# Flamingo block on one core: the seam between attention and experts, re-ordered by halves

## The chip, the cores and the metric

The kernel runs on 1 core of a Trainium2 chip. The metric is the device time of one execution in microseconds (us), taken as the median of several runs. The engines are TensorE (PE in the profile; PEld are its weight loads), VectorE (DVE), ScalarE (ACT), GpSimd (POOL) and SyncE (SP), which issues most DMAs.

## The reference, cut to what matters

```python
# x, ctx: (16, 256, 512); Wq (512, 512), Wkv (512, 1024); 8 experts, w1, w2, w3: (8, 512, 512)
x = x + tanh(g_xattn) * attention(layernorm(x) @ Wq, ctx @ Wkv)        # one head, softmax over 256 keys
xn = layernorm(x)
probs = softmax(xn @ gate_w + gate_b, axis=1)                          # over the TOKENS of a batch
vals, idx = top_k(probs, 2)                                            # two best experts of each token
y = relu(relu(relu(xn @ w1[e] + b1[e]) @ w2[e] + b2[e]) @ w3[e] + b3[e])
v[e, o] = sum over tokens of y * vals where e is chosen                # per batch and expert, see below
out = sum over chosen e of v[e]                                        # v sums over all 16 batches
x = x + tanh(g_ffn) * out
```

All products are computed in about full float32 precision: each operand is split into a high part (rounded by ScalarE, names `..._hi`) and a low part (`..._lo`, the rest, a subtraction), and three matmuls (hi·hi, hi·lo, lo·hi) are added up in PSUM.

## The kernel before

**Attention phase.** It runs as a software pipeline over 16 batches of 256 tokens. In step b each engine works on several batches at once: `scores(b)`, `gate_transposes(b-2)`, `values(b)`, `ranks(b-2)`, `xn2_transposes(b-1)`, `x_times_a(b+1)`, `gate_logits(b-1)`, `p_times_v(b)`. The gate of a batch is a chain over engines: `gate_logits` (PE), `gate_softmax` (DVE, with the exponential `gate_exp` on ACT), `gate_transposes` (PE), `two_best` (DVE: the two best experts of each token), `ranks` (PE), `slots` (DVE: the slot of each token in its expert's list), `send_pairs` (POOL: four indirect DMAs that write (token, weight) pairs to DRAM).

**Expert phase.** The tokens are taken in tiles of 352 rows that all belong to one expert. For each tile the rows' indices are loaded (`load_idx`, SP), the rows are gathered (`gather`, POOL, three indirect DMAs), transposed on PE (`row_transposes`) into `et`, split (`et_high` on ACT, `et_low` on DVE), and run through three layers (`layer1_half`, `layer2_half`, `layer3_half`: two halves of 24 matmuls of 352 columns each), with `relu_half` on ACT between them and `h_lo` as the low part of the hidden rows. Weights are split once for each tile: `split_w` on ACT, `w_low` on DVE, each over 128x2048 elements. From tile 2 on the tiles run in a loop.

**The table.** Which expert and which rows a tile has is worked out by DVE from the running counts: an early table for 8 tiles once 12 batches are counted (`early_table`, in step 14, 15 dependent steps), the full one in `full_table` (20 steps). The engines read it with a register load (`tiles_in_use`).

**The seam.** The order of every engine between the last attention step and the tile loop is written out by hand. PE: `scores(15)`, `gate_transposes(13)`, `values(15)` with `ranks(13)` inside, `pt_transposes(15)`, `xn2_transposes(14)`, `row_transposes(0)`, `p_times_v(15)`, `gate_logits(14)`, `layer1_half(0, 0)`, `gate_transposes(14)`, `layer1_half(0, 1)`, `row_transposes(1)`, `layer2_first()`, `ranks(14)`, `xn2_transposes(15)`, `layer2_half(0, 1)`, `gate_logits(15)`, `layer1_half(1, ·)`, `gate_transposes(15)`, `row_transposes(2)`, `layer3_half(0, 0)`, `ranks(15)`, `layer3_half(0, 1)`. An engine never overtakes: it waits on semaphores in this order. In DVE's list, `et_low(0)`, `w_low(0, 0)`, `gate_softmax(14)`, `attended(15)`, `w_low(1, 0)`, `two_best(14)`, `et_low(1)`, `slots(14)`, `w_low(0, 1)`, `gt_low(15)`, `w_low(2, 0)`, `gate_softmax(15)`, `w_low(1, 1)` follow one another. In POOL's list stand `gather(1)`, `send_pairs(13)`, `norm2_scale(15)`, `h_low(0, 0)`, `gather(2)`, `send_pairs(14)`, `h_low(1, 0)`, `h_low(0, 1)`. `norm2_scale(15)` gives ScalarE the factors for `norm2(15)`, behind which stand `et_high(1)` and `split_w(0, 1)`.

Before the attention phase the product of Wq and Wk is formed in four steps over c: PE waits for `wq_hi`, `wk_hi`, then for `wq_lo` (DVE), `wk_lo` (POOL). Its matmul lines are 1350 (hi·hi) and 1355, 1356. DVE's line 933 is the helper `low` (every subtraction that gives a low part); PE's lines 1321 to 1323 are the helper `split_product`; 1521 to 1523 are `layer2_first`; 1335 `xn2_transposes`; 1393 `ranks`; 1443 `gate_logits`; 1461 `gate_transposes`; 1576 `row_transposes`.

## Time and profile before

| | |
|---|---|
| median of 3 runs | 938.21 us (937.06 to 938.34) |
| the profiled execution | 939.05 us, its span 937.2 us |
| PE busy | 914.1 us, 98% of the span |
| DVE, ACT, POOL busy | 716.1, 496.1, 277.3 us |
| mean granted TensorE clock | 0.984 |

The span runs from the first to the last instruction; the profiled execution's own time is 1.85 us longer. A row of a timeline gives start, duration, engine, line and operation, then what is written and read, and in brackets the engine's idle time before it with what ended it. Rows whose matmuls overlap are counted by their starts: one begins every 0.16 us at full clock for 352 columns. "Granted clock" 1.00 is 2.4 GHz, 0.50 is 1.2 GHz.

### The profile page before, as it was taken

The page shows a single profiled execution, that of the slowest core. Times are in us where ns is not written, and L with a number is a line of the kernel's source. Part 1 is how long each engine was busy: PE and PEld are TensorE (multiplying, and loading weights), DVE is VectorE, ACT ScalarE, POOL GpSimd, SP SyncE. Part 2 cuts the span into 40 slices and gives each one's busy share as a digit, 9 for nine tenths or more (in the row PEclk, how much of TensorE's full clock was granted, in tenths as well). Part 3 has the DMA queues.
Part 4 walks back from the last instruction along what each step waited for, and adds up shares of the span by engine and source line. Part 5 has one row for each costly group of instructions (what it writes and reads, how often), then busy time and mean ns, then how long its engine had stood idle before and what let it go on. Part 6 is the DMA issues. An engine that isn't in the chain of part 4 may idle for free.

```text
span 937.2 us, 18798 instructions
## 1 busy us (share of the span) xinstructions
PE 914.1 (98%) x5746; PEld 861.3 (92%) x5746; DVE 716.1 (76%) x1369; ACT 496.1 (53%) x690; POOL 277.3 (30%) x316
## 2 busy tenths in 40 slices
PE   9999999999999989999999999999999999999985
PEld 6989988889989878999999999999999999999981
DVE  5667877888778876977777777777777777777756
ACT  5345444454444366556666666666666666666521
POOL 4224444435454557743211111111111111110003
PEclk9999999999999998999999999999999999999995
DMA  7423232223322354447866789973663653752009
GB/s 237 158 100 126 98 128 90 90 98 126 102 99 68 96 148 115 109 124 208 217 206 161 200 239 249 255 224 108 153 198 108 158 192 108 179 172 78 17 17 358
DMA packets 91925, 138.68 MB, mean 148 GB/s; under 512 B 28528, under 2 KB 56944, under 8 KB 88688
## 3 DMA queue, kind: packets, MB, share of 16 engines
q1 hardware_dynamic: 84464, 120.86, 43.1%
q0 software_dynamic: 7424, 17.38, 7.0%
q8 instruction: 18, 0.29, 0.1%
q14 instruction: 19, 0.16, 0.1%
HBM read 106.66 MB, written 31.53 MB: 147 GB/s over the span
## 4 chain that ended last, share of the span: by engine, by line
PE 88%; DVE 4%; DMA 2%; issue 2%; POOL 2%; ACT 1%; SPq 0%; DVEq 0%; POOLq 0%; ACTq 0%
PE bank L1321 27%; PE bank L1322 27%; PE bank L1323 27%; DVE x_all L1311 2%; PE bank L1335 1%; PE bank L1404 1%; DMA xg<-xn_dram,idx 1%; DMA idx<-slot_pair 1%; PE bank L1445 1%; DMA wq_raw<-in_wq_t 1%; POOL slot_pair L634 1%; PE bank L1447 0%; POOL xg L664 0%; DVE probs L1018 0%; PE bank L1576 0%
## 5 line engine op out<-in xcount | busy, mean ns | idle before, releaser
L1321 PE MATMUL bank<-h_hi,w_hi 128*128 128x352 f32 x744 | 241.4, 324 | 1.1 <-issue 1.1
L1323 PE MATMUL bank<-h_hi,w_lo 128*128 128x352 f32 x744 | 240.1, 323 | 0.0
L1322 PE MATMUL bank<-h_lo,w_hi 128*128 128x352 f32 x744 | 239.1, 321 | 0.0
L664 POOL DMA_INDIRECT xg<-xn_dram,idx x72 | 89.6, 1244 | 361.6 <-DMA idx<-slot_pair 346.4
L933 DVE TENSOR_TENSOR w_lo<-w_raw,w_hi 128x2048 fp32r<-128x2048 f32 x72 | 166.4, 2310 | 23.3 <-ACT w_hi L821 18.8
L832 ACT ACTIVATE h<-bank,bias 128x352 f32<-128x352 f32 x192 | 95.8, 551 | 141.5 <-PE bank L1323 139.8
L821 ACT ACTIVATE w_hi<-w_raw 128x2048 fp32r<-128x2048 f32 x72 | 137.4, 1909 | 36.4 <-PE bank L1323 33.0
L1321 PEld LDWEIGHTS bank<-h_hi,w_hi 128*128 128x128 f32 x744 | 139.8, 188 | 1.5 <-issue 1.4
L933 DVE TENSOR_TENSOR h_lo<-h,h_hi 128x704 fp32r<-128x704 f32 x86 | 76.3, 888 | 83.6 <-ACT h_hi L838 83.5
L1322 PEld LDWEIGHTS bank<-h_lo,w_hi 128*128 128x128 f32 x744 | 139.7, 188 | 0.0
L1323 PEld LDWEIGHTS bank<-h_hi,w_lo 128*128 128x128 f32 x744 | 139.3, 187 | 0.0
L1321 PE MATMUL bank<-et_hi,w_hi 128*128 128x352 f32 x384 | 124.0, 323 | 1.3 <-DVE et_lo L933 1.3
L1322 PE MATMUL bank<-et_lo,w_hi 128*128 128x352 f32 x384 | 123.0, 320 | 0.0
L1323 PE MATMUL bank<-et_hi,w_lo 128*128 128x352 f32 x384 | 123.0, 320 | 0.0
L634 POOL DMA_INDIRECT slot_pair<-pair,slot_u x64 | 69.2, 1082 | 40.2 <-DVE pair L990 23.3
L838 ACT ACTIVATE h_hi<-h 128x704 fp32r<-128x704 f32 x96 | 76.3, 794 | 5.5 <-PE bank L1447 1.7
L1321 PEld LDWEIGHTS bank<-et_hi,w_hi 128*128 128x128 f32 x384 | 72.0, 188 | 1.6 <-DVE w_lo L933 1.6
L1322 PEld LDWEIGHTS bank<-et_lo,w_hi 128*128 128x128 f32 x384 | 72.1, 188 | 0.0
L1323 PEld LDWEIGHTS bank<-et_hi,w_lo 128*128 128x128 f32 x384 | 72.0, 187 | 0.0
L1321 PE MATMUL bank<-xt_hi,a_hi 128*128 128x256 f32 x240 | 69.1, 288 | 0.0
L1323 PE MATMUL bank<-xt_hi,a_lo 128*128 128x256 f32 x240 | 67.9, 283 | 0.0
L1322 PE MATMUL bank<-xt_lo,a_hi 128*128 128x256 f32 x240 | 67.9, 283 | 0.0
(215 smaller groups left out, 1735.6 us busy)
## 6 DMA issues: line engine op xcount, KB each, us to landing
w_raw<-in_w SPq DMA_DIRECT2D x24, 1024.0 KB, 5.2
xq<-rows_dram SPq DMA_DIRECT2D x80, 176.0 KB
w_raw<-in_w SPq DMA_DIRECT2D x48, 256.0 KB, 6.7
rows_dram<-xg SPq DMA_DIRECT2D x20, 512.0 KB, 3.3
wb<-slot_pair SPq DMA_DIRECT2D x24, 352.0 KB, 4.0
xt_raw<-in_x_t SPq DMA_DIRECT2D x16, 512.0 KB, 4.0
c_raw<-in_ctx_t SPq DMA_DIRECT2D x16, 512.0 KB, 3.4
x_all<-in_x SPq DMA_DIRECT2D x16, 512.0 KB, 4.5
```

The source lines that it names most:

```text
L634: pool.indirect_dma_start(slot_pair, bass.IndirectOffsetOnAxis(ap=slot_u[:, k, n:n + 1], axis=0), pair[:, k, n], None).then_inc(pair_sent[ ...
L664: pool.indirect_dma_start(xg[0:n, c], None, rows, bass.IndirectOffsetOnAxis(ap=idx[0:n, c, 0:1], axis=0)).then_inc(gathered, 16)
L821: act.activation(w_hi[n][:], w_raw[n][:], ACT.Copy).then_inc(w_his[n], 1)
L832: act.activation(h[:, oc], layer_banks(n, m)[oc][:, 0:TILE], ACT.Relu, bias=bias[n][:, oc:oc + 1]).then_inc(relu_done[n], 1)
L838: act.activation(h_hi[n][:, 2 * k:2 * k + 2], h[:, 2 * k:2 * k + 2], ACT.Copy).then_inc(h_his[n], 1)
L933: dve.tensor_tensor(dst, src, hi.bitcast(F32), ALU.subtract).then_inc(done, 1)
L1311: dve.tensor_tensor(row, bank[n % 8][:], row, ALU.add).then_inc(res_dve, 1)
L1321: pe.matmul(out_ap, lh, rh, start=(i == 0), stop=False)
L1322: pe.matmul(out_ap, lh, rl, start=False, stop=False)
L1323: last = pe.matmul(out_ap, ll, rh, start=False, stop=(i == n - 1))
L1335: last = pe.transpose(banks[dc // 2][:, (dc % 2) * S + c * P:(dc % 2) * S + (c + 1) * P], src[:, c, dc * P:(dc + 1) * P], ident[:])
L1404: last = pe.transpose(bS[:, k * S + c * P:k * S + (c + 1) * P], pexp[:, c, k * P:(k + 1) * P], ident[:])
```

## The change

1. **Seam, tile 0.** `h_low(0, 0)` moves from POOL to DVE (`h_rest`). w1 and w2 of tile 0 are split by halves of the contraction: `split_first_w` on ACT (w1 only), `first_w_low` on DVE (w1 and w2). `layer1_half(0, 0)` becomes `layer1_first`, which goes through the contraction by halves, as `layer2_first` did, and both wait for a half at a time. DVE's `w_low(1, 0)`, then, is `first_w_low(1, 0)`, `h_rest` half 0, `first_w_low(1, 1)`, `h_rest` half 1.
2. **PSUM banks.** Layer 1 of tile 0 uses bank 6 in place of 3, `row_transposes(1)` bank 3 in place of 6, and the waits follow.
3. **Gate.** The biased low logits (`logit_low`) are made by ACT (`gate_low`), the maximum comes out negated in one step, and `two_best` reads PSUM itself and compares the integer indices: 6 steps for 8. This holds for all batches.
4. **Tables.** `early_table` stands behind `two_best(12)` and has 11 steps for 15, `full_table` 17 for 20; three constant tables are made at the start of the kernel on DVE.
5. **Tile 3.** `et_low(3)` stands ahead of `w_low(0, 3)`.
6. **Start.** ScalarE makes `wk_hi[n]` before `wq_hi[n]`.

```diff
         def layer_banks(n, m):
-            first = {(0, 0): (0, 1, 2, 3), (0, 1): (4, 5, 6, 0), (1, 0): (0, 1, 2, 3),
+            first = {(0, 0): (0, 1, 2, 6), (0, 1): (4, 5, 6, 0), (1, 0): (0, 1, 2, 3),
...
-            first = {0: (1, 2, 0), 1: (4, 5, 6), 2: (1, 2, 3)}
+            first = {0: (1, 2, 0), 1: (4, 5, 3), 2: (1, 2, 3)}
...
@@ POOL, seam
             norm2_scale(B - 1)
-            h_low(0, 0)
             gather(2)
...
@@ ACT
+            def gate_low(m):
+                act.wait_ge(gate_done, m + 1)
+                act.activation(logit_low[:], R_LOGIT_LOW, ACT.Identity, bias=gb[:, 0:1]).then_inc(gate_low_done, 1)
...
                 if exists(b - 1, B):
+                    gate_low(b - 1)
                     gate_exp(b - 1)
...
             for n in range(DC):
+                act.wait_ge(s_wk_in[n], 16)
+                act.activation(wk_hi[:, n], wk_raw[:, n], ACT.Copy).then_inc(s_wk_hi, 1)
                 act.wait_ge(s_wq_mean, n + 1)
                 act.activation(wq_hi[:, n], wq_raw[:, n], ACT.Identity, bias=wq_mean[:, n, 1:2]).then_inc(s_wq_hi, 1)
-                act.wait_ge(s_wk_in[n], 16)
-                act.activation(wk_hi[:, n], wk_raw[:, n], ACT.Copy).then_inc(s_wk_hi, 1)
...
+            def split_first_w(k):
+
+                act.wait_ge(w_in[0], W_IN[0])
+                act.activation(w_hi[0][:, 2 * k:2 * k + 2], w_raw[0][:, 2 * k:2 * k + 2], ACT.Copy
+                               ).then_inc(w_first_hi if k == 0 else w_his[0], 1)
...
             et_high(0, range(2))
-            split_w(0, 0)
+            split_first_w(0)
             et_high(0, range(2, TH))
+            split_first_w(1)
+            gate_low(B - 2)
             gate_exp(B - 2)
...
             split_w(1, 1)
+            gate_low(B - 1)
             gate_exp(B - 1)
...
@@ DVE, gate_softmax
-                need(dve, gate_done, m + 1)
-                dve.tensor_scalar(logit_low[:], R_LOGIT_LOW, gb[:, 0:1], None, ALU.add).then_inc(gate_step, 1)
-                dve.wait_ge(gate_step, 3 * m + 1)
+                dve.wait_ge(gate_low_done, m + 1)
                 dve.tensor_tensor(logit[:], R_LOGIT, logit_low[:], ALU.add).then_inc(gate_step, 1)
...
+                dve.tensor_reduce(gmax[:], logit[:], AX_X, ALU.max, negate=True).then_inc(gmax_ready, 1)
...
@@ DVE, step 14
-                if isinstance(b, int) and b == KNOWN + 2:
-                    early_table()
                 if exists(b - 2, B):
                     two_best(b - 2)
+                if isinstance(b, int) and b == KNOWN + 2:
+                    early_table()
...
@@ DVE, seam
+            def first_w_low(n, k):
+
+                dve.wait_ge(w_first_hi if (n, k) == (0, 0) else w_his[n], 1)
+                low(w_lo[n][:, 2 * k:2 * k + 2], w_raw[n][:, 2 * k:2 * k + 2], w_hi[n][:, 2 * k:2 * k + 2],
+                    w_first_lo if k == 0 else w_los[n])
...
             et_low(0, range(2))
-            w_low(0, 0)
+            first_w_low(0, 0)
             et_low(0, range(2, TH))
+            first_w_low(0, 1)
             gate_softmax(B - 2)
             attended(B - 1)
-            w_low(1, 0)
+            first_w_low(1, 0)
+            h_rest(0, 0, [0])
+            first_w_low(1, 1)
+            h_rest(0, 0, [1])
             two_best(B - 2)
...
             w_low(1, 2)
+            et_low(3)
             w_low(0, 3)
-            et_low(3)
...
@@ PE
+            def layer1_first():
+
+                need(pe, et_los, TH)
+                for k in range(2):
+                    pe.wait_ge(w_first_lo if k == 0 else w_los[0], 1)
+                    for oc in range(2):
+                        z = layer_banks(0, 0)[oc][:, 0:TILE]
+                        rows = slice(oc * P, (oc + 1) * P)
+                        for i in range(2 * k, 2 * k + 2):
+                            pe.matmul(z, w_hi[0][:, i, rows], et_hi[:, i], start=(i == 0), stop=False)
+                            pe.matmul(z, w_hi[0][:, i, rows], et_lo[:, i], start=False, stop=False)
+                            last = pe.matmul(z, w_lo[0][:, i, rows], et_hi[:, i], start=False, stop=(i == DC - 1))
+                last.then_inc(l_done[0], 1)
...
             gate_logits(B - 2)
-            layer1_half(0, 0)
+            layer1_first()
             gate_transposes(B - 2)
             layer1_half(0, 1)
```

## Rows read from the trace of the kernel before

**Rows 1.** Busy time by stretch: PE, PEld, DVE, ACT, POOL; granted clock, DMA share, GB/s.

```profile
320.00:360.00 40.00, 35.48 (x206) 31.85 (x204) 26.76 (x76) 19.68 (x32) 24.08 (x26) 0.91 0.62 170
...
480.00:880.00 400.00, 400.00 (x2500) 400.00 (x2499) 312.25 (x388) 243.56 (x279) 56.45 (x48) 1.00 0.61 170
```

**Rows 2.** Timeline of the kernel's start: DVE, PE.

```profile
7.58 0.69 DVE L1162 TENSOR_REDUCE wq_mean<-wq_raw 128x1 f32<-128x512 f32 x1 [0.80 <-DMA wq_raw<-in_wq_t]
...
11.30 0.47 PE L1355 MATMUL bank<-wk_lo,wq_hi 128*128 128x512 f32 x1 [0.22 <-POOL wk_lo L679]
```

**Rows 3.** Timeline of attention step 14: DVE's table and two best, then PE's ranks.

```profile
305.86 0.16 DVE L1106 TENSOR_TENSOR cnt<-base,ebase 128x8 f32<-128x8 f32 x1
...
309.32 0.17 DVE L1039 COPY pr<-bank 128x16 f32<-128x16 f32 x1
...
311.15 0.18 PE L1393 MATMUL bank<-ind,tri_half 128*128 128x16 bf16 x1 [1.24 <-DVE ind L1056]
```

**Rows 4.** Timeline of PE in the seam.

```profile
339.60 0.41 PE L1321 MATMUL bank<-et_hi,w_hi 128*128 128x352 f32 x1 [1.34 <-DVE et_lo L933]
...
347.77 1.58 PE L1576 MATMUL bank<-ident,xg 128*128 128x128 f32 x12
352.53 0.63 PE L1521 MATMUL bank<-h_hi,w_hi 128*128 128x352 f32 x1 [3.18 <-POOL h_lo L674]
...
357.65 0.48 PE L1523 MATMUL bank<-h_hi,w_lo 128*128 128x352 f32 x1
...
359.29 1.09 PE L1335 MATMUL bank<-ident,xn 128*128 128x128 f32 x8
...
364.40 0.31 PE L1443 MATMUL bank<-gt_hi,gw 128*40 128x256 f32 x1 [0.20 <-DVE gt_lo L933]
...
373.64 0.26 PE L1461 MATMUL bank<-ident,probs 8*128 8x8 f32 x2 [0.48 <-DVE probs L1018]
```

**Rows 5.** Busy time of PE by single microseconds, with the granted clock after it.

```profile
351.00:352.00 1.00, 0.00 (x0) 0.58 0.00 0
...
357.00:358.00 1.00, 1.00 (x5) 0.51 0.79 249
```

**Rows 6.** Timeline of DVE in the seam.

```profile
336.70 2.29 DVE L933 TENSOR_TENSOR w_lo<-w_raw,w_hi 128x2048 fp32r<-128x2048 f32 x1 [0.56 <-ACT w_hi L821]
...
345.78 2.26 DVE L933 TENSOR_TENSOR w_lo<-w_raw,w_hi 128x2048 fp32r<-128x2048 f32 x1
...
352.83 1.75 DVE L933 TENSOR_TENSOR et_lo<-bank,et_hi 128x512 fp32r<-128x512 f32 x3 [3.13 <-ACT et_hi L854]
...
363.06 1.28 DVE L933 TENSOR_TENSOR gt_lo<-bank,gt_hi 128x512 fp32r<-128x512 f32 x2
...
366.57 0.47 DVE L1008 TENSOR_SCALAR logit_low<-bank,gb 8x256 f32<-8x256 f32 x1
...
370.63 2.86 DVE L1018 TENSOR_SCALAR probs<-gexp,gsum 8x256 f32<-8x256 f32 x1
```

**Rows 7.** The page, part 5: three groups (busy us, mean ns | idle before, releaser).

```profile
L832 ACT ACTIVATE h<-bank,bias 128x352 f32<-128x352 f32 x192 | 95.8, 551 | 141.5 <-PE bank L1323 139.8
L821 ACT ACTIVATE w_hi<-w_raw 128x2048 fp32r<-128x2048 f32 x72 | 137.4, 1909 | 36.4 <-PE bank L1323 33.0
...
L933 DVE TENSOR_TENSOR h_lo<-h,h_hi 128x704 fp32r<-128x704 f32 x86 | 76.3, 888 | 83.6 <-ACT h_hi L838 83.5
```

**Rows 8.** Timeline of ACT in the seam.

```profile
349.00 0.79 ACT L838 ACTIVATE h_hi<-h 128x704 fp32r<-128x704 f32 x1
```

**Rows 9.** Timeline of POOL in the seam.

```profile
345.37 0.97 POOL L634 DMA_INDIRECT slot_pair<-pair,slot_u  x1 [0.30 <-issue]
346.64 2.24 POOL L634 DMA_INDIRECT slot_pair<-pair,slot_u  x1 [0.30 <-issue]
...
350.71 3.32 POOL L674 TENSOR_TENSOR h_lo<-h,h_hi 128x704 fp32r<-128x704 f32 x2
```

**Rows 10.** Waits of PE between 300 and 480 us: total, times, longest.

```profile
PE bank L1321 <- issue: 1.1, 1, 1.1
```

More of the change, by code:

```diff
@@ L920, in _ @@
             dve.wait_ge(s_conv, 5)
+            for n, less in enumerate((TILE, 1)):
+                dve.scalar_tensor_tensor(out=thr_e[:, n], in0=thr[:].unsqueeze(1).broadcast_to([P, E, TILES_MAX]),
+                                         scalar=float(less), in1=ebase[:].unsqueeze(2).broadcast_to([P, E, TILES_MAX]),
+                                         op0=ALU.add, op1=ALU.add).then_inc(s_conv, 1)
+            dve.tensor_scalar(first_row[:], jidx[:], float(TILE), None, ALU.mult).then_inc(s_conv, 1)
+            dve.wait_ge(s_conv, 8)
             def stats(src_batch, st, mv, done, step_sem_base):
@@ L1061, in batch @@
                     exp_bias(b)
+                if exists(b - 2, B):
+                    two_best(b - 2)
                 if isinstance(b, int) and b == KNOWN + 2:
                     early_table()
-                if exists(b - 2, B):
-                    two_best(b - 2)
                 if exists(b + 1, B):
@@ L1114, in write_table @@
                 rows = slice(first, first + n)
-                do(dve.tensor_scalar(row2[:, 0:n], row1[:, 0:n], float(TILE), None, ALU.mult))
-                do(dve.scalar_tensor_tensor(out=row3[:, 0:n], in0=tile_e[:, rows], scalar=float(REGION),
-                                            in1=row2[:, 0:n], op0=ALU.mult, op1=ALU.add))
+                do(dve.scalar_tensor_tensor(out=table[:, rows, 1], in0=tile_e[:, rows], scalar=float(REGION),
+                                            in1=row1[:, 0:n], op0=ALU.mult, op1=ALU.add))
                 do(dve.tensor_copy(table[:, rows, 0], tile_e[:, rows]))
-                do(dve.tensor_copy(table[:, rows, 1], row3[:, 0:n]))
                 do(dve.tensor_tensor(tile_onehot[:, :, rows], tile_e[:, rows].unsqueeze(1).broadcast_to([P, E, n]),
@@ L1128, in do @@
                     link(ins, early_step, step)
-                count_tiles(do, ntile[:], TILE)
+                count_tiles(do, ntile[:], 0)
                 tile_list(do, 0, EARLY, ntile[:, 0:E - 1])
@@ L1203, in et_low, with h_rest @@
                         et_hi[:, :, a:a + n], et_los)
-            def h_rest(n, m):
-                for k in range(2):
+            def h_rest(n, m, halves=range(2)):
+                for k in halves:
                     dve.wait_ge(h_his[n], 2 * m + k + 1)
@@ L1500, in layer1_half @@
                 if isinstance(m, int) and m == 0:
-                    if k == 1:
-                        need(pe, x2_done, RC * B - 1)
+                    need(pe, gt_los, 2 * (B - 1))
                 elif isinstance(m, int) and m == 1:
@@ L1512, in layer2_first @@
             def layer2_first():
-                need(pe, w_los[1], 1)
                 for k in range(2):
+                    pe.wait_ge(w_first_lo if k == 0 else w_los[1], 2 - k)
                     need(pe, h_los[0], k + 1)
@@ L1528, in layer2_half @@
                 need(pe, h_los[0], 2 * (m + 1))
-                if not (isinstance(m, int) and m == 0):
-                    if isinstance(m, int):
-                        need(pe, et_los, TH * (m + 2))
-                    need(pe, relu_done[1], DC * m)
+                if isinstance(m, int):
+                    need(pe, et_los, TH * (m + 2))
+                need(pe, relu_done[1], DC * m)
                 if isinstance(m, int) and m == 1:
```

62 lines of the change are left out of this document (27 added, 35 removed).

## The prediction

> **What bounds the kernel now.** I read the busy time by stretch first. From 480 to 880 us PE is busy for 400.00 of 400 us, and so it is in nearly all of the attention phase: the kernel is bound by PE's matmuls, whose number the change leaves alone. What can be won is PE's idle time and its time at the low clock. Between 320 and 360 us PE is busy for 35.48 of 40 us, at a mean granted clock of 0.91 [rows 1]. The list of waits and PE's timeline give the holes one by one. Ahead of the seam there is 1.24 us before `ranks(12)` [rows 3]. In the seam there are 1.34 us before layer 1 of tile 0, 3.18 us before `layer2_first`, 0.20 before `gate_logits(15)` and 0.48 before `gate_transposes(15)` [rows 4]; later 1.1 us of "issue", PE's register load of the table [rows 10]. The reader is to see in the rows by single microseconds that the clock went to 0.50 in microsecond 351, with PE idle, and was still 0.51 in microsecond 357, with PE busy [rows 5]: some 6.8 us at the low level. Half of them, 3.4 of 40 us, is about what the mean of 0.91 lacks, so it was the one fall of this stretch. The 3.18 us wait has thus a second price. Then I followed DVE, ACT and POOL through the same time to see what would be late next.
>
> All times below are those of the old trace; what moves as a whole stays at its old time until the sum.
>
> **Start.** PE is held by the split weights: in the second of four steps it waits 0.22 us for `wk_lo`, after DVE had waited for the DMA of `wq_raw` until 7.58 [rows 2]. With `wk_hi` first, POOL starts on `wk_lo` up to one ScalarE copy (some 0.6 us) earlier in each step, and PE could run some 0.9 us ahead by the end of the four steps. Against it, `wq_hi` comes behind a copy that may itself wait for its DMA, and DVE makes three small tables first (three steps of some 0.25 us, beside the DMA wait). No row shows when `wk_raw` lands. Bounds: nothing (all eaten by the DMAs) and 0.9; I take 0.4, near the middle, since the DMA is still the first releaser.
>
> **Step 14.** The early table takes DVE from 305.86 to 309.32, 15 steps, 0.23 each, and `two_best(12)`, 8 steps, ends behind it just ahead of PE's `ranks` at 311.15, which waited 1.24 us for it [rows 3]. With `two_best` first, in 6 steps, it ends near 307.2, when PE is still in `values(14)`: the 1.24 us go. The table, with 11 steps, ends near 309.8 in place of 309.3, but DVE's list as a whole is 1.2 us shorter, so `xt_low(15)` and everything behind keep pace with PE. Gain 1.24. In the other steps PE is full, so the gate's shorter chain is worth nothing there.
>
> **Seam, layer 1.** DVE is free at 336.14 (336.70 less 0.56). Half a `w_low` is 1.15 us, one `et_low` of three 0.58 [rows 6], so both are done by 337.9. PE ends `gate_logits(14)` at 338.26 (339.60 less 1.34): no wait, gain 1.34. The second half is there at 339.0, needed at 340.2.
>
> **Seam, layer 2.** `row_transposes(1)` begins at 347.77 - 1.34 = 346.43 and PE can start `layer2_first` at 347.9. The low h was POOL's, and POOL took it up only at 350.71, behind its DMAs and `norm2_scale` [rows 9]. Now DVE makes it. `gate_softmax(14)` is about 0.75 us shorter (`logit_low`, 0.47 [rows 6], the negation, two gaps), so DVE comes to w2 at 345.0 and not 345.78 [rows 6]. Then 1.15 for a half of w2 and 0.89 for a half of h [rows 7] give 347.05: in time. For the second half, `h_hi` ends at 349.79 [rows 8] less 1.34, so 348.45; plus 0.1 and 0.89 that is 349.4, against PE's need at 349.8. The 3.18 us go, by 0.4 us of margin. With them goes the low clock: the 18 matmuls from 352.53 on start 0.30 us apart (357.65 is the start of the last [rows 4]), where 2500 in 400 us are 0.16 [rows 1]: 18 times 0.14 is 2.5 us, of which I count 2.4. So PE would come to `xn2_transposes(15)` at 359.29 - 1.34 - 3.18 - 2.4 = 352.4.
>
> **What is late next.** That product needs `xn2` and two thirds of `et_low(1)`, because it shares banks 4 and 5. Their chain is not shortened: POOL's `gather(1)` and `send_pairs(13)`, `norm2_scale(15)` until 350.7 [rows 9], then ACT's `norm2(15)` and `et_high(1)`, then `et_low(1)`, which waited for ACT until 352.83 and takes 1.75: two of three chunks done at 354.1 [rows 6]. PE waits 1.7 us here, and the gain at this point is 359.29 - 354.1 = 5.2. How the DMAs of `send_pairs` fare decides: one took 0.97 us while DVE read PSUM or one operand, the next 2.24, ending 0.9 us after DVE's `w_low` of 345.78 had ended [rows 6, 9]. In the new order DVE's halves and `h_rest` follow each other from 345.0 to 349.3. If POOL gets in between two of them, `send_pairs` ends at 347.0 to 349.1 (348.9 before), and the result above holds within 0.6 us.
>
> Next, `gt_low(15)`: DVE goes from the end of `et_low(1)`, 354.6, through `slots(14)` and `w_low(0, 1)`, together 3.7 us (from 359.3, when `ranks` was done, to 363.06), to `gt_low` (1.28) [rows 4, 6], done at 359.6; PE arrives 4.9 us after 354.1 (364.20 less 359.29), at 359.0. It waits 0.6; the gain is 364.40 - 359.65 = 4.75 [rows 4]. Then `gate_transposes(15)`: PE arrives 8.76 us later (373.16 less 364.40), at 368.4. `gate_low(15)` stands on ACT behind `split_w(1, 1)`, and DVE's logits wait for it, where before they were ready at 366.57 ahead of it [rows 6]. ACT's h of layer 2 waits for `gate_logits(15)`, done near 360.8; then come `h_hi` 0.8 [rows 8], two relus 1.1, `h_hi` 0.8, the split 1.9 [rows 7], with overlaps 365.2. With 0.45 for each of `gate_low`, the sum, the maximum and the exponential (as `logit_low`, 0.47), small steps and gaps of 0.1 to 0.2, `probs` is there at 368.0, before PE. If POOL is then in its `h_low(1, 0)`, where one h half takes it 1.66 us [rows 9], it can be 369.05: `probs` took 2.86 us in the old trace, for as many elements as the 0.47 [rows 6]. The gain is 5.24 or 4.6; I take 4.9, the middle. DVE idles 361.8 to 365.7 for this, but its `w_low(1, 1)` is needed only at 378.
>
> Tile 3's `et_low`, moved ahead of `w_low(0, 3)`, is waited for by PE before the register load; the load itself cost 1.1 us [rows 10]. Bounds of what an earlier `et_low(3)` hides: 0 and 1.1; I take 0, since the row puts it down to no other engine. From there PE is full again [rows 1].
>
> **Sum.** 0.4 + 1.24 + 4.9 = 6.5 us of the profiled execution's 939.05, so 932.5; the median of the runs shown is 0.8 lower, 938.21, and gives **931.7 us**. That PE has no hole which this case needs but the 1.7 and 0.6 us is its weak place. Its own range is 930.6 to 932.4, from the start's bounds and the two ends at `probs`.
>
> **Rivals.**
> A. *The new wait costs the clock as the old one did.* PE would do only `ranks` and then transposes for some 3 us around the wait of 1.7. For it: the clock fell within 2 us of the last transpose before 352 [rows 4, 5]. Against it: waits of 1.24 and 1.34 us did not lower it. Price: up to the 2.4 us of before, less the 0.6 at `gt_low` that now lie beneath; at half that number of matmuls 0.6. Middle 1.2: 932.9, up to 933.5. The Trainium skill ("TensorE: Matmul & The Clock Gate", Part 4) states that PE-mode transposes do not count as PE being busy. By it this rival is the likelier one; the trace agrees so far as the fall came with transposes and a wait behind each other.
>
> B. *POOL is held up less than before.* Were its last DMA of 2.24 us one of 0.97 [rows 9], `et_low(1)` would be there at 352.85, `gt_low` at 358.4, and the gain at the seam some 6.2: 938.21 - 7.8 = 930.4. It takes luck in the order of arrival. The Trainium skill ("SBUF — State Buffer", Who interferes with whom) infers that DVE's `tensor_tensor` does not hold up POOL's descriptor writing. By it this rival would be certain; the 2.24 us speak against it.
>
> C. *POOL is held up throughout.* If it does not get in between DVE's halves, its last DMAs wait until 349.3, `norm2_scale` ends 2.3 us later, the wait grows to 4.0 and the clock falls as before: 6.5 - 2.3 - 1.8 = 2.4 gained, 935.8.
>
> D. *Nothing of it reaches the seam's end* because other chains (rows of tile 1, w2) hold PE where it was; only step 14 remains: 937.0. `gather(1)` and both weights were there without a wait, so little speaks for it.
>
> E. *Slower: the clock stays low.* At 1.2 GHz about 0.46 us are lost in each microsecond (0.14 of 0.30). Three waits behind each other, at 354, 359 and 368, could keep it low. It takes 14 us at the low level to annul the 6.5, 18 to be slower by 0.2%; from 352 to 374 it would be 22 us, 9.5 lost, 941.2. The low stretch before was under 7 us.
>
> **Chances.** Forecast 0.45, A 0.29, B 0.11, C 0.07, D 0.04, E 0.04. The range 929.8 to 934.8 holds the first three cases with the bounds of the start (0.5 more) and of the register load's partly hidden 1.1 us, 0.85 in all. 0.2% is 1.9 us, about what a measurement tells from no change: faster (forecast, A, B and C) 0.92, within it 0.05, slower 0.03.
>
> **What the profile after would show.** `ranks(12)` without a wait; layer 1 of tile 0 without one; `layer2_first` right behind `row_transposes(1)` at 1.00; a wait of 1 to 2.5 us before `xn2_transposes(15)` ended by `et_lo`; then one under 1 us for `gt_lo`, and a small one for `probs`; the granted clock in that stretch decides between forecast and A, POOL's DMAs of `send_pairs(13)` between forecast, B and C. It would be wrong if `gate_low` came later on ACT than I work out, or if the 0.4 us of margin at the second half of h were not there.

## The result

The changed kernel took 929.98 us (median of 4 runs, 929.80 to 930.19), the kernel before 938.28 beside it (4 runs). The ratio is 0.9914, 95% interval 0.9897 to 0.9931: 8.3 us faster, where 6.5 were forecast. The time is inside the range of 929.8 to 934.8, 0.2 us above its low end, and 0.6 us below the range that the forecast gave to its own case. The profiled execution took 929.86, with a span of 928.1 against 937.2.

The seam's stretch as in [rows 1], busy time of PE, PEld, DVE, ACT and POOL, then granted clock, DMA share and GB/s:

```profile
320.00:360.00 40.00, 38.25 (x245) 34.63 (x244) 31.91 (x78) 25.15 (x41) 24.25 (x24) 1.00 0.64 165
```

PE gained 2.8 us of busy time between 320 and 360, and the clock is whole. PE's timeline after, for the places of [rows 2 to 4]:

```profile
6.88 1.20 PE L1368 MATMUL bank<-wk_hi,wq_hi 128*128 128x512 f32 x4 [1.11 <-ACT wq_hi L806]
...
309.03 0.18 PE L1411 MATMUL bank<-ind,tri_half 128*128 128x16 bf16 x1
...
328.52 0.18 PE L1411 MATMUL bank<-ind,tri_half 128*128 128x16 bf16 x1 [0.74 <-DVE ind L1067]
...
336.85 0.32 PE L1524 MATMUL bank<-et_hi,w_hi 128*128 128x352 f32 x1
...
348.98 0.40 PE L1552 MATMUL bank<-h_hi,w_hi 128*128 128x352 f32 x1 [0.54 <-DVE h_lo L952]
351.56 0.63 PE L1353 MATMUL bank<-ident,xn 128*128 128x128 f32 x4 [0.16 <-issue]
...
356.79 0.31 PE L1461 MATMUL bank<-gt_hi,gw 128*40 128x256 f32 x1 [0.30 <-DVE gt_lo L952]
...
366.03 0.26 PE L1479 MATMUL bank<-ident,probs 8*128 8x8 f32 x2 [0.49 <-DVE probs L1033]
```

The reader is to see that `ranks(12)` (309.03) and layer 1 of tile 0 (336.85) have no wait, that the wait of 3.18 us for h became one of 0.54, at its second half, and that only 0.16 us stand before `xn2_transposes(15)` (351.56), where 1.7 were expected. At 328.52 there is a new wait of 0.74 us that no step of the prediction has. DVE (POOL and ACT below it) tells why:

```profile
305.90 0.21 DVE L1067 TENSOR_TENSOR ind<-oh 128x48 bf16<-128x48 f32 x1
308.41 0.23 DVE L1127 TENSOR_TENSOR tile_onehot<-tile_e,iota_e 128x64 f32<-128x64 f32 x1
...
326.38 0.69 DVE L960 TENSOR_REDUCE smax<-bank 128x2 f32<-128x512 f32 x1 [2.54 <-remote]
...
344.43 0.89 DVE L952 TENSOR_TENSOR h_lo<-h,h_hi 128x704 fp32r<-128x704 f32 x1
347.94 0.89 DVE L952 TENSOR_TENSOR h_lo<-h,h_hi 128x704 fp32r<-128x704 f32 x1 [1.50 <-ACT h_hi L847]
350.12 1.75 DVE L952 TENSOR_TENSOR et_lo<-bank,et_hi 128x512 fp32r<-128x512 f32 x3
...
364.55 1.33 DVE L1033 TENSOR_SCALAR probs<-gexp,gsum 8x256 f32<-8x256 f32 x1
```

```profile
335.27 1.73 POOL L663 DMA_INDIRECT xg<-xn_dram,idx  x1 [8.54 <-DMA idx<-slot_pair]
343.87 1.49 POOL L633 DMA_INDIRECT slot_pair<-pair,slot_u  x1 [0.30 <-issue]
347.86 0.19 POOL L619 TENSOR_TENSOR rn<-rn 128x2 f32<-128x2 f32 x1
```

```profile
348.09 1.52 ACT L777 ACTIVATE xn<-x_all,rn 128x512 f32<-128x512 f32 x2 [0.18 <-POOL rn L619]
362.34 0.47 ACT L765 ACTIVATE logit_low<-bank,gb 8x256 f32<-8x256 f32 x1
```

Up to `gate_transposes(12)` the marks of this trace come 0.68 us sooner than in the old one; with that added `two_best(12)` ends at 306.8 and the table at 309.3, 0.4 and 0.5 us ahead of the forecast. DVE stood still for 2.54 us before 326.38, and the profile names no engine as releaser ("remote"). `send_pairs(13)`'s last DMA took 1.49 us, not 2.24 [rows 9], and `gate_low(15)` came at 362.34, 5.55 us after `gate_logits(15)`, just as the prediction had it (365.2 less 359.65).

**Where the 9.1 us of span came from.** I compared the distances between PE's marks, so that an offset at one place is not counted at the next. The change is worth:

| stretch of PE's timeline | before | after | gain |
|---|---|---|---|
| to `gate_transposes(0)` | 64.14 | 63.88 | 0.26 |
| from there to `gate_transposes(12)` | 239.78 | 239.36 | 0.42 |
| to `ranks(12)` | 7.23 | 5.79 | 1.44 |
| to `gate_transposes(13)` | 14.15 | 14.16 | -0.01 |
| to `ranks(15)` (the seam) | 53.98 | 48.47 | 5.51 |
| to `row_transposes(3)` | 19.63 | 19.60 | 0.03 |
| to the end's transposes of v | 513.22 | 511.70 | 1.52 |
| to the end | 25.07 | 25.14 | -0.07 |

Step 14 and the seam are as forecast within 0.6 us, and that with 0.85 us lost in the seam to DVE's stop (from `gate_transposes(13)` to `ranks(13)` it is 5.33 us, before 4.48). 1.5 us came at a place that the prediction put at nothing; its rows are shown with experiment 3.

### The profile page after: what moved, and what is told of

Its sections match the earlier page's. It is cut to its first block, busy times and chain, and to the rows that moved or that the text cites. A ratio compares the mean times of both kernels' runs of the same rounds, so it can differ in the third digit from the quotient of the medians.

```text
span 928.1 us, 18701 instructions
## 1 busy us (share of the span) xinstructions
PE 909.5 (98%) x5746; PEld 858.4 (92%) x5746; DVE 694.9 (75%) x1305; ACT 503.5 (54%) x707; POOL 276.2 (30%) x314
## 4 chain that ended last, share of the span: by engine, by line
PE 91%; DVE 3%; issue 1%; POOL 1%; DMA 1%; SPq 1%; ACT 1%; DVEq 0%; POOLq 0%; ACTq 0%
PE bank L1339 28%; PE bank L1341 28%; PE bank L1340 28%; DVE x_all L1329 2%; PE bank L1353 1%; PE bank L1422 1%; PE bank L1463 1%; PE bank L1465 1%; DMA idx<-slot_pair 0%; POOL slot_pair L633 0%; DMA wk_raw<-in_wk_t 0%; PE bank L1373 0%; PE bank L1479 0%; PE bank L1606 0%; PE bank L1414 0%
## 5 line engine op out<-in xcount | busy, mean ns | idle before, releaser
L663 POOL DMA_INDIRECT xg<-xn_dram,idx x72 | 93.0, 1291 | 359.3 <-DMA idx<-slot_pair 343.6
L952 DVE TENSOR_TENSOR w_lo<-w_raw,w_hi 128x2048 fp32r<-128x2048 f32 (+1 forms) x74 | 166.5, 2250 | 23.8 <-ACT w_hi L824 18.7
L824 ACT ACTIVATE w_hi<-w_raw 128x2048 fp32r<-128x2048 f32 x71 | 135.5, 1908 | 35.5 <-PE bank L1341 33.1
L1339 PE MATMUL bank<-et_hi,w_hi 128*128 128x352 f32 x376 | 121.4, 323 | 0.0
L1340 PE MATMUL bank<-et_lo,w_hi 128*128 128x352 f32 x376 | 120.4, 320 | 0.0
L1341 PE MATMUL bank<-et_hi,w_lo 128*128 128x352 f32 x376 | 120.3, 320 | 0.0
```

Source lines behind the costliest of these rows:

```text
L663: pool.indirect_dma_start(xg[0:n, c], None, rows, bass.IndirectOffsetOnAxis(ap=idx[0:n, c, 0:1], axis=0)).then_inc(gathered, 16)
L824: act.activation(w_hi[n][:], w_raw[n][:], ACT.Copy).then_inc(w_his[n], 1)
L952: dve.tensor_tensor(dst, src, hi.bitcast(F32), ALU.subtract).then_inc(done, 1)
L1339: pe.matmul(out_ap, lh, rh, start=(i == 0), stop=False)
L1340: pe.matmul(out_ap, lh, rl, start=False, stop=False)
L1341: last = pe.matmul(out_ap, ll, rh, start=False, stop=(i == n - 1))
```

## The experiments

Each kernel is the changed one with the edit shown; where not said otherwise the rest is as it is. "The seam" is the distance from `gate_transposes(13)` to `ranks(15)`, 48.47 us in the changed kernel.

**1. Low h of tile 0 back on POOL.**

```
 DVE: first_w_low(1, 0)
-     h_rest(0, 0, [0])
      first_w_low(1, 1)
-     h_rest(0, 0, [1])
 POOL: norm2_scale(B - 1)
+      h_low(0, 0)
       gather(2)
```

> The changed kernel with one part undone: the low h of tile 0 is made by POOL again, w1 and w2 stay in halves. Theory 1 (the move to DVE removed the 3.18 us wait): that wait comes back, with the low clock behind it, 3.2 + 2.4 = 5 us or more over the 929.98 of the changed kernel, near 935. Theory 2 (the halves let POOL finish its DMAs early, and POOL would have been in time): norm2_scale ends near 348 as in the changed kernel, POOL's first half of h is there at 349.7, PE waits under 1.5 us at layer2_first, the clock stays at 1.00, and the time is 0.3 to 1.2 us above 929.98.

Measured: 933.63 us (5 runs, 932.79 to 935.11), ratio 0.9955 (0.9940 to 0.9970), 3.6 us over the changed kernel. The kernel before took 938.02 us beside this one; by the ratios the two changed kernels are 0.41% apart, 3.9 us, and the intervals do not touch. PE's timeline, PE busy and granted clock by single microseconds, and POOL:

```profile
349.07 0.40 PE L1551 MATMUL bank<-h_hi,w_hi 128*128 128x352 f32 x1 [3.77 <-POOL h_lo L673]
```

```profile
350.00:351.00 1.00, 1.00 (x5) 0.50 0.99 406
```

```profile
347.26 3.33 POOL L673 TENSOR_TENSOR h_lo<-h,h_hi 128x704 fp32r<-128x704 f32 x2
```

POOL takes h up at 347.26, PE waits 3.77 us and starts at half the clock. The seam is 51.94 us. So the move to DVE takes away the wait of 3.2 to 3.8 us together with its fall of the clock: theory 1 in kind. The price is under the 5 us that it named. The low clock lasted about 3.4 us here and 6.8 before, by the granted clock of the single microseconds. And the kernels with h on DVE that stand below, in 2 and 3, have a wait of their own at `xn2_transposes(15)`; their seams are only 2.3 and 2.4 us shorter than this one.

**2. The early table ahead of the two best, in its short form.**

```
+                if isinstance(b, int) and b == KNOWN + 2:
+                    early_table()
                 if exists(b - 2, B):
                     two_best(b - 2)
-                if isinstance(b, int) and b == KNOWN + 2:
-                    early_table()
```

> The changed kernel with the early table ahead of two_best(12) again, in its short form. Theory 1 (the order removed the 1.24 us wait): PE waits about 1 us at ranks(12) again. Theory 2 (shortening by 4 and 2 steps, some 1.25 us, was enough): PE waits 0 to 0.2 us at ranks(12), time within 0.3 us of 929.98.

Measured: 930.74 us (929.13 to 931.13), ratio 0.9919 (0.9901 to 0.9937). From `gate_transposes(12)` to `ranks(12)` it is 5.79 us, as in the changed kernel: shortening the two lists was enough, and the order adds nothing (theory 2). What is new is at the seam (PE, then its clock, then POOL):

```profile
352.21 1.50 PE L1353 MATMUL bank<-ident,xn 128*128 128x128 f32 x8 [2.37 <-DVE et_lo L952]
```

```profile
352.00:353.00 1.00, 0.79 (x6) 0.85 0.75 299
353.00:354.00 1.00, 1.00 (x6) 0.50 0.98 400
```

```profile
336.64 1.19 POOL L663 DMA_INDIRECT xg<-xn_dram,idx  x1 [9.77 <-DMA idx<-slot_pair]
348.51 0.19 POOL L619 TENSOR_TENSOR rn<-rn 128x2 f32<-128x2 f32 x1
```

Here PE does wait for `et_lo`, 2.37 us, and the clock falls while it transposes. DVE had no stop before this and PE no wait at `ranks(13)`; tile 1's gather began at 336.64, and POOL's norm scale ended at 348.70. The granted clock was whole again from microsecond 356 on (0.95). The seam is 49.60 us, a gain of 4.38. This is the mechanism of the prediction's rival A, though the time, 930.74 us, is not its 932.9. Yet the edit does not touch the seam: what differs here differs between executions.

**3. Tile 3's rows behind its w1.**

```
-            et_low(3)
             w_low(0, 3)
+            et_low(3)
```

> The changed kernel with et_low(3) behind w_low(0, 3) again. Theory 1 (the register load's 1.1 us before the loop are hidden because PE's sequencer no longer stands at the wait for et_low(3)): a wait of 1.0 to 1.2 us put down to issue comes back before the loop's first matmul, +1.0 us. Theory 2 (it vanished for another reason, such as the earlier full table): no wait, no difference.

Measured: 932.26 us (930.17 to 933.06), ratio 0.9934 (0.9913 to 0.9955). The seam is as in the run before (2.37 us for `et_lo`, 49.58). Behind `row_transposes(3)` it loses 0.76 us (512.46 against 511.70), 0.3 of it a wait for `part`; no "issue" wait is there. So neither theory holds as it stands: the wait of theory 1 is absent, and there is a difference where theory 2 has none. DVE is done with `et_low(3)` here at 400.96, some 1.3 us before PE comes by; in the old trace the two met at 408.2. DVE in this run, then DVE and PE in the kernel before, then DVE in the changed kernel:

```profile
399.21 1.75 DVE L952 TENSOR_TENSOR et_lo<-bank,et_hi 128x512 fp32r<-128x512 f32 x3
```

```profile
406.43 1.74 DVE L933 TENSOR_TENSOR et_lo<-bank,et_hi 128x512 fp32r<-128x512 f32 x3
409.46 0.42 PE L1321 MATMUL bank<-h_hi,w_hi 128*128 128x352 f32 x1 [1.14 <-issue]
```

```profile
395.66 1.75 DVE L952 TENSOR_TENSOR et_lo<-bank,et_hi 128x512 fp32r<-128x512 f32 x3 [2.09 <-ACT et_hi L863]
```

At this one place, the loop's first matmul of PE, the kernel before loses 1.44 of its 1.52 us against the changed kernel; experiment 3, with the old order, loses 0.06 there and the rest of its 0.76 in the next 30 us.

**4. w1 and w2 of tile 0 whole, h on DVE.** `split_w`, `w_low` and `layer1_half` in place of the halves; DVE: `w_low(1, 0)`, then `h_rest(0, 0)`.

> The changed kernel with w1 and w2 of tile 0 split whole again on both engines, and layer 1's first half as before; the low h stays on DVE. Theory 1 (my forecast: the move of h is the main gain, the halves are worth the 1.34 us of layer 1): +1.3 us, and the wait before xn2_transposes(15) under 0.5 us. Theory 2 (the halves set POOL free): besides the 1.3 us, the DMAs of gather(1) and send_pairs(13) that meet a w_low take 2.2 us again, norm2_scale(15) ends 1.2 to 2.5 us later, and PE waits 1.5 to 2.5 us before xn2_transposes(15): +2.5 to +3.5 us, more if the clock falls.

Measured: 930.64 us (930.51 to 932.55), ratio 0.9923 (0.9906 to 0.9939).

```profile
338.69 0.40 PE L1336 MATMUL bank<-et_hi,w_hi 128*128 128x352 f32 x1 [1.30 <-DVE w_lo L951]
353.81 1.06 PE L1350 MATMUL bank<-ident,xn 128*128 128x128 f32 x8 [1.29 <-DVE et_lo L951]
```

```profile
344.50 2.70 POOL L633 DMA_INDIRECT slot_pair<-pair,slot_u  x1 [0.30 <-DVE mv L948]
```

```profile
344.10 2.26 DVE L951 TENSOR_TENSOR w_lo<-w_raw,w_hi 128x2048 fp32r<-128x2048 f32 x1
```

Theory 1 named 1.3 us more and theory 2 at least 2.5; by medians it is 0.7, and nothing against 2 and 3. The whole w1 does cost 1.30 us at layer 1. But PE then waits 1.29 us, not 2.37, for `et_lo`, since it comes there later, and the clock stays at 1.00: the seam is 49.43, no longer than in 2 and 3. With POOL's chain as late as this the halves gain nothing; what they bring PE is waited away at `et_lo`. The rows of POOL and DVE show the price of POOL's DMAs: one took 2.70 us beside a `w_lo` from 344.10 to 346.36 and was done 0.84 us after it.

**5. POOL's norm scale one DMA sooner.**

```
-            send_pairs(B - 3, (B - 3) % 2)
+            send_pairs(B - 3, (B - 3) % 2, range(3))
             norm2_scale(B - 1)
+            send_pairs(B - 3, (B - 3) % 2, range(3, 4))
```

> The changed kernel with batch 15's norm scale on POOL put one indirect transfer sooner, ahead of the last of send_pairs(13). Theory 1: the wait for et_lo at xn2_transposes(15), 2.37 us with a clock fall in two earlier runs, is set by the chain POOL scale, ACT norm2, ACT et_hi, DVE et_lo. Then the scale ends near 346.3 instead of 348.1 to 348.7, norm2 follows h_hi at once, PE waits under 0.7 us there, the clock stays at 1.00 from 340 to 360, and the time is 929.3 (928.6 to 930.0). Theory 2: the second half of h, on ACT and DVE, sets it as much; then the wait moves to layer2_first's second half or stays at 1 us or more, and the time is the changed kernel's, 930.0 to 930.8.

**6. The gate of batch 15 ahead of the split of w2 on ACT.**

```
             relu(1, 0)
-            split_w(1, 1)
             gate_low(B - 1)
             gate_exp(B - 1)
+            split_w(1, 1)
```

> The changed kernel with the gate of batch 15 (its low logits and its exp on ACT) ahead of the split of tile 1's w2. Theory 1: the 0.49 us that PE waits for probs at gate_transposes(15) comes from gate_low standing behind that split; the wait goes and the time is 929.5 (929.0 to 930.0). Theory 2: the split is now late for DVE, whose w_low then holds up two_best(15) and ranks(15); the wait reappears there or at layer 2 of tile 1 with 0.3 us or more, and the time is 930.0 to 930.6.

**7. The old order at the start**: on ACT `wq_hi` ahead of `wk_hi` in each of the four steps.

> The changed kernel with the old order on ACT at the start, Wq's half ahead of Wk's. Theory 1: the start's gain was the 0.2 us wait for wk_lo and a little of the chain, 0.4 us in all; counted from PE's first Wk times Wq matmul, the attention of batch 0 is reached 0.4 to 0.5 us later than in the changed kernel, and the time is 930.4 (930.0 to 930.9). Theory 2: the start is set by when the weights land, and the order is worth nothing: same distance within 0.1 us, and the time is 930.0 within 0.4.

**8. Nothing but the shorter gate, two best and table**: the edits of 1, 3, 4 and 7 together.

> The changed kernel without what its title names: low h of tile 0 on POOL, w1 and w2 whole, tile 3's rows last, the old start. What is left is the shorter gate, two best and early table, with the table behind the two best. Theory 1: the parts add up; 1.24 us at step 14 and 0.4 to 0.6 us over the steps leave 936.6 (936.0 to 937.2). Theory 2: the shorter DVE chain also lets PE's seam start sooner, so that the waits for w_lo and h_lo there shrink or grow: then PE's waits for h_lo at layer2_first are other than 3.2 us, by what the time differs from 936.6.

Measured: 928.56 us for 5 (928.31 to 930.62; ratio 0.9906, 0.9889 to 0.9922), 929.88 for 6 (928.55 to 930.42; 0.9914, 0.9898 to 0.9931), 931.04 for 7 (930.20 to 931.34; 0.9924, 0.9907 to 0.9940), 936.78 for 8 (10 runs, 934.13 to 937.91; 0.9981, 0.9971 to 0.9990). The intervals of 5, 6 and 7 overlap with each other and with the changed kernel's: what these edits do is read from the profiles, one for each, and not from the medians. All four show DVE's stop of 2.4 us before `smax(15)` and a wait of 0.6 us at `ranks(13)`, as the changed kernel's profile does.

5 and 7 make the pair that decides on the chain of `et_lo`, since tile 1's gather begins at the same time in both. POOL and PE of 5, then of 7:

```profile
335.42 1.20 POOL L663 DMA_INDIRECT xg<-xn_dram,idx  x1 [8.93 <-DMA idx<-slot_pair]
346.24 0.19 POOL L619 TENSOR_TENSOR rn<-rn 128x2 f32<-128x2 f32 x1
```

```profile
350.16 1.09 PE L1354 MATMUL bank<-ident,xn 128*128 128x128 f32 x8
```

```profile
335.50 1.21 POOL L663 DMA_INDIRECT xg<-xn_dram,idx  x1 [8.91 <-DMA idx<-slot_pair]
347.59 0.91 POOL L619 TENSOR_TENSOR rn<-rn 128x2 f32<-128x2 f32 x1
```

```profile
348.59 0.40 PE L1552 MATMUL bank<-h_hi,w_hi 128*128 128x352 f32 x1 [0.44 <-DVE h_lo L952]
352.01 1.06 PE L1353 MATMUL bank<-ident,xn 128*128 128x128 f32 x8 [0.98 <-DVE et_lo L952]
```

With the scale ending at 346.43 PE waits for nothing; with 348.50 it waits 0.44 us for h and 0.98 for `et_lo`. The seams are 47.16 and 49.07 us. Theory 1 of experiment 5 holds in the profile: the chain from POOL's scale sets that wait.

The start: counted from PE's first matmul of Wk and Wq, `gate_transposes(0)` comes 57.05 us later in 7 and 57.00 in the changed kernel, so behind that mark the order is worth nothing that can be seen (theory 2). The old trace has 57.48: there the second piece of Wq landed 0.7 us later, DVE beginning on it at 7.58 [rows 2] and in experiment 7 at 6.85. In experiment 8, also with the old order, DVE begins at 7.17, and the distance is 57.08.

The mark itself is not free of the order, though. With the old order (before, 7, 8) that first matmul began at 6.66 or 6.67 us each time. With the new one ScalarE's first work is `wk_hi`, for whose DMA it waited 3.1 to 4.8 us in all eleven profiles, `wq_hi` stands behind it, and the matmul began between 6.48 and 8.13. `gate_transposes(0)` came at 63.72 and 63.74 in 7 and 8 and at 63.58 to 65.17 in the eleven. So no gain of the new order is seen, and a loss in some executions is not excluded.

Of the 0.9 us by which 7's profiled execution is longer than the changed kernel's, 0.60 stand at the seam, with the chain, and 0.44 behind the end's transposes of v; none of it is the edit's.

Experiment 6: the gate came sooner, and PE waited all the same. DVE, POOL and PE:

```profile
361.18 3.14 DVE L1033 TENSOR_SCALAR probs<-gexp,gsum 8x256 f32<-8x256 f32 x1
```

```profile
360.80 3.37 POOL L673 TENSOR_TENSOR h_lo<-h,h_hi 128x704 fp32r<-128x704 f32 x2
```

```profile
364.47 0.26 PE L1479 MATMUL bank<-ident,probs 8*128 8x8 f32 x2 [0.40 <-DVE probs L1033]
```

`probs` began 5.96 us after `gate_logits(15)`, 1.8 us sooner than in the changed kernel, and took 3.14 us, for it lay beside POOL's subtractions of h and ended 0.15 us after them. Neither theory had it.

Experiment 8's time is what theory 1 said, though by other terms. Its seam is 53.98 us, that of before to the hundredth, with 3.67 us for h_lo, 1.31 for w_lo and the clock at half. DVE's stop costs it 0.7 us there, so the edits that it keeps must give 0.7 back; which of them does was not tried. Behind `row_transposes(3)` it needs 513.96 us, 2.26 more than the changed kernel and 0.74 more than the kernel before, where experiment 3 needed 0.76 more with the same order. PE's waits from 385 us on:

```profile
PE bank L1335 <- DVE part L1243: 1.3, 1, 1.3
PE bank L1335 <- issue: 0.4, 1, 0.4
```

So about half of the gain behind tile 3 comes with the seam, as far as one profile of each can say: where the seam is short, as in 3, only 0.76 us hang on the order of `et_low(3)`, 0.06 of them at the loop's first matmul; where it is not, as in 8, PE has the two waits shown.

**9. The changed kernel once more; 10. tile 1's indices loaded ahead of w2; 11. edit 6 with tile 0's second low h on DVE.** Edits of 10 and 11:

```
 SP:  load_w(0, 0)
+     load_idx(1)
      load_w(1, 0)
      for n in range(3):
          load_b(n, 0)
-     load_idx(1)
```

```
 POOL: send_pairs(B - 2, (B - 2) % 2)
-      h_low(1, 0)
+      pool.wait_ge(xn2_out, 16 * B)
 DVE:  w_low(2, 0)
+      dve.wait_ge(xn2_out, 16 * B)
+      h_rest(1, 0)
       gate_softmax(B - 1)
```

> The changed kernel once more, beside the next two on one chip. In five profiles of it and its variants DVE stands still for 2.4 to 2.5 us at 323.5, before smax(15), with no engine named, and PE waits 0.6 to 0.7 us for ind at step 15; in four others neither is there. Theory 1: this belongs to the run's place, not to the code; then here it is in all three kernels that leave SP's order alone or in none, and the time is 929.9 to 930.8. Theory 2: it varies from one execution to the next; then the times of single runs lie in two groups about 1 us apart.

> The changed kernel with SP's load of tile 1's indices ahead of the loads of w2 and the biases. Theory 1: POOL's work at the seam starts when the indices have landed (334.3 to 336.6), and this landing time is late since the index load queues behind 1 MB of w2; then gather(1) starts by 334.3, POOL's rn ends by 346.3, PE waits under 0.3 us for h_lo and et_lo, the clock stays at 1.00, and the time is 929.0 (928.4 to 929.8). Theory 2: gather(1) is held by something else, PE's reading of the rows of tile 0 or the transfers themselves; then it starts within 0.5 us of the kernel run beside it and the time is the same. Theory 3: w2 lands later, ACT's split of it is late, and PE waits for w_lo at layer2_first, 0.5 us or more.

> The changed kernel with batch 15's gate ahead of the split of tile 1's w2 on ACT, as in the run before, and tile 0's second low h on DVE in place of POOL. Theory 1: with the gate sooner, DVE's probs took 3.14 us in place of 1.33, since it ran beside POOL's subtractions of h; with these gone it takes 0.5 us, the wait of 0.4 to 0.5 us at gate_transposes(15) goes, and the time is 0.4 us (0.2 to 0.9) under the changed kernel's beside it. Theory 2: POOL's subtractions are not what lengthens it; probs stays over 1.3 us and the wait stays. Theory 3: the gate is no longer late, but DVE's extra 1.8 us makes another wait of PE, for ind or w_lo, of 0.3 us or more.

Measured: 929.46 us for 9 (928.58 to 930.72; ratio 0.9907, 0.9890 to 0.9923), 928.61 for 10 (928.33 to 930.28; 0.9900, 0.9883 to 0.9916), 929.65 for 11 (929.36 to 930.18; 0.9904, 0.9887 to 0.9920). POOL's first gather of tile 1 and the end of its scale in 9, then the gather in 10:

```profile
334.17 1.10 POOL L663 DMA_INDIRECT xg<-xn_dram,idx  x1 [7.68 <-DMA idx<-slot_pair]
346.29 0.20 POOL L619 TENSOR_TENSOR rn<-rn 128x2 f32<-128x2 f32 x1
```

```profile
333.72 1.10 POOL L663 DMA_INDIRECT xg<-xn_dram,idx  x1 [7.17 <-PE bank L1606]
```

DVE's stop was there in all three (2.41, 2.33 and 2.38 us), and absent in experiments 1 to 4, which have the same code there and ran beside each other on one chip: theory 1 of 9 for the stop. Theory 2 is not excluded for the rest, since the single times of 9 (928.58, 928.72, 930.20, 930.72) do lie in two groups. In 9 POOL's gather starts 1.1 us sooner than in the changed kernel's first profile and PE waits neither for h nor for `et_lo`; the seam is 47.37 us. In 10 the gather waits for PE's reading of tile 0's rows and no longer for the indices; the wait for `probs` is gone too (the seam is 46.69 us). Theory 1 of 10 holds in the profile; 0.85 us of medians are within the spread of the runs. Experiment 11's profile has a stop of ACT, with "remote" behind it again, in which PE waits 1.32 us for h. Its median is not under that of 9, as theory 1 had it, and behind `row_transposes(3)` it loses 0.36 us. But its gate says what was asked: `probs` takes 0.34 us, PE waits for nothing there, and from `gate_logits(15)` to `gate_transposes(15)` it is 8.69 us in place of 9.27. ACT and DVE:

```profile
344.85 1.00 ACT L841 ACTIVATE h<-bank,bias 128x352 f32<-128x352 f32 x2 [4.04 <-remote]
```

```profile
363.52 0.34 DVE L1033 TENSOR_SCALAR probs<-gexp,gsum 8x256 f32<-8x256 f32 x1
```

**12. The edits of 10 and 11 together.**

> The changed kernel with three edits together: SP's index load of tile 1 ahead of w2, batch 15's gate ahead of the split of tile 1's w2, and tile 0's second low h on DVE. Theory 1: they meet different waits, h_lo and et_lo at the seam and probs at gate_transposes(15), so the gains add up: no wait of PE above 0.3 us from 330 to 400, ranks(15) by 369.6, and the time is 928.2 (927.6 to 929.0), 10 us under the kernel before. Theory 2: the seam's gain of the index load already took the 0.4 us wait for probs with it, since POOL is through with h sooner, and DVE's extra work is only in the way: 928.6 to 929.4, no better than the index load alone.

Measured: 928.04 us (4 runs, 927.93 to 928.47), before 937.68 beside it; ratio 0.9897 (0.9881 to 0.9914): 9.6 us faster than before, the best median of all, on theory 1's number. All of PE's waits of 0.3 us or more in the whole span:

```profile
PE bank L1663 <- DVE v L1322: 2.6, 1, 2.6
PE bank L1365 <- POOL zeros L580: 1.2, 1, 1.2
PE bank L1370 <- ACT wq_hi L806: 0.9, 1, 0.9
PE bank L1413 <- DVE ind L1067: 0.5, 1, 0.5
PE bank L1673 <- DVE v L1324: 0.5, 1, 0.5
PE bank L1463 <- DVE gt_lo L952: 0.4, 1, 0.4
```

In the seam 0.4 us for `gt_lo` are left; the rest are the two ends and DVE's stop (`ind`). `ranks(15)` came at 370.03, 0.4 later than theory 1 wanted, 0.2 of it from the start. That it beats 10 by 0.6 us is not certain: the ratios' intervals overlap.

## Why the prediction was right, and where it was not

That the time fell into the range is in part luck. Of the 9.1 us of span 2.6 were not in the sum, DVE's stop took back 0.85 us that no step had, and the range held by 0.2 us, with the help of a bound that was put in for the register load. The forecast's own range, 930.6 to 932.4, was missed; by the bounds that it names its lower end would have been 930.9. Of the numbers given, rival B's 930.4 lies nearest. (In rival E, 22 us at the low clock would cost 10.1 us at 0.46, not 9.5.)

**Start (forecast 0.4, measured 0.26, due to the order nothing that is seen).** The term is wrong in kind. Experiment 7 undoes the order, and `gate_transposes(0)` comes no later. What the old trace lost behind PE's first matmul is, as far as three profiles with the old order can say, a late DMA of that one execution: where DVE began on Wq's second piece at 7.58, 7.17 and 6.85 (before, 8, 7), the distance is 57.48, 57.08 and 57.05. The lower bound, "all eaten by the DMAs", was the right value, and the prediction named the reason: `wq_hi` now comes behind a copy that waits for its own DMA.

**Step 14 (1.24, measured 1.44).** Right in place and size. Its reason was half right: the order does not matter (experiment 2), the shorter lists do. The table's 11 steps took 0.24 us each, where 0.23 had been put down. All was 0.4 to 0.5 us ahead of the forecast because DVE, offset taken off, came to `two_best` at 305.5, 0.3 us sooner than it had begun the table before.

**In the other steps (nothing, measured 0.42).** From `gate_transposes(0)` to `(12)` each step is 0.035 us shorter, in all twelve experiments alike, 8 included. The matmuls that follow `gate_transposes` start slightly closer. Which of the shared edits does it was not tried.

**Layer 1 (1.34).** The wait went, as forecast, and DVE had both halves in time. But experiment 4 shows that as long as `et_lo` holds PE later, this gain is not kept.

**Layer 2 and the clock (3.18 and 2.4).** Right in kind: experiment 1 gives 3.77 us of wait back, and a clock of 0.50 for half as long as before. The term of 2.4 us measured 2.5: from the start of `layer2_first` to `xn2_transposes(15)` it is 4.27 us in 9, which waits for nothing there, against 6.76 before. The margin at the second half, put at 0.4 us, was there in 2 to 6, 9, 10 and 12 (no wait) and missing by 0.54 in the first profile, by 0.44 in 7.

**The new wait at `xn2_transposes(15)` (1.7 us).** The step named the right wait and the right chain, and its size is one of a spread: 0.16 us in the first profile, 0 in 5, 6, 9, 10 and 12, 0.98 in 7, 1.29 in 4, 2.37 in 2 and 3. The chain's end was well put where the forecast's conditions held: two thirds of `et_low(1)` were to be there 28.8 us after `gate_transposes(13)`, and PE went on at 28.9 in 2 and 3. PE's arrival, 27.1 by the prediction's terms, looks right in 9 with 27.24, but that holds 0.7 us of DVE's stop; without the stop, in 2 and 3, PE came at 26.5. Hence 2.37 and not 1.7. What I took for a fixed number, the old trace's POOL chain, moves with the landing of tile 1's indices: the gather began 12.42 us after that mark before, 13.2 to 13.7 us in 1 to 4, 12.08 in the changed kernel's first profile, 11.2 to 12.5 in 5 to 9 and 11, 10.7 with the indices ahead of w2. Among the kernels with h on DVE the wait follows it. The exceptions are 5, with its scale moved, and 4 and 11, where PE comes late for another reason. Rival A (0.29) is what 2 and 3 show, rival B's mechanism (POOL held up less) what the first profile and 9 show. The forecast lay between the two.

**A's price.** In 2 the distance from `xn2_transposes(15)` to `gate_logits(15)` is 6.32 us against 5.23 in the changed kernel: 1.1 us net for the clock, where the prediction had 1.2 in the middle. The wait for `gt_lo` behind it was gone, and that for `probs` too. The granted clock went to 0.50 after 2.37 us of waiting with `ranks` before and transposes after it; it did not after 1.29 us at the same place (4), nor after 0.98 (7). The Trainium skill ("TensorE: Matmul & The Clock Gate", Part 4) has it that transposes do not count as PE being busy in the same way. Experiments 2 and 3 agree with it as far as they go, but the length of the wait alone, 2.37 us against 1.34 at most, tells them apart as well; the transposes of `xn2` and of tile 0's rows, back to back from 330.43 on in 9, went by at 1.00.

**POOL's DMAs.** The prediction left open if POOL gets in between two of DVE's halves. By the traces it does: the last of `send_pairs(13)` ran from 343.87 to 345.36 in the changed kernel, 0.85 after the first half of w2 had ended, although `h_lo` followed it at once. Rival C did not occur in any run. The Trainium skill ("SBUF — State Buffer", Who interferes with whom) infers the opposite, that DVE's `tensor_tensor` leaves descriptor writing alone. The 2.70 us of experiment 4 against 0.97 for its neighbour speak against it. The same section says that `tensor_scalar` can enter a mode with two ports, and that it and POOL then shut each other out, the one that issued first holding the pair for its whole instruction. The 3.14 us for `probs` in 6 against 0.34 in 11 agree with it in kind; but `probs` came behind two subtractions of POOL, not one, and ended 0.15 us after the second.

**gt_lo and probs (0.6, and 0 to 0.65).** Measured 0.30 and 0.49. The seam's 4.9 became 5.51, with 6.6 in 9 and 4.4 in 2. What varies in it is the 1.7 us and DVE's stop, which costs PE 0.6 to 0.85 us and which no step had.

**The register load and tile 3 (0, bounds 0 and 1.1; measured 1.5).** This is the step that failed. I took "issue" at its word: a wait that no engine ends. In the old trace DVE ended `et_low(3)` at 408.17, PE was through with tile 1's matmuls at 408.3 and went on at 409.46. With `et_low(3)` done at 397.4 there is no such hole, nor in 3 with 400.96; in 8, where it is done at 405.08, 0.39 us are left. In the two profiles with a hole PE goes on 1.29 and 1.32 us after `et_low(3)` is done, and in 3, where it closes, the matmul begins 1.33 us after. So the price depends on when DVE is done, and that comes at least as much from the shorter seam and the shorter lists as from the new place of `et_low(3)`: with the old place, 3 has no hole and 8 a third of it. That the load hides beneath queued matmuls when the wait ahead of it is over early is my reading of these four; it was not tried by itself. Of the 2.6 us by which the gain in span (9.1) exceeds the sum (6.5), 1.5 are this step.

**Chances.** The kernel is faster, to which 0.92 was given. Nothing spoke for D or E. The new PSUM banks are in every kernel of the experiments, so their part was not tried.

## What to carry to other kernels

When a wait is taken away, the next wait's size is set by a chain on other engines that did not move; look for what starts this chain (here a small load of indices queued behind 1 MB of weights) and treat it as a spread, not as the one number that one trace shows. An "issue" wait of PE that follows a wait for another engine's product is to be read together with when that product was done. Before work is handed to an engine because it idles, see what runs beside it: two subtractions on POOL turned 0.34 us of DVE into 3.14. And where a mark is chosen to measure from, see that the edit does not move the mark.
